# Work of a routed attention's start moved into the two stages before it, and its one-hots spread tile by tile in its loop

## The chip, the cores and the metric

The kernel runs on one core of one Trainium2 chip. The metric is the device time of one execution in microseconds (us). Engines: PE (TensorE), DVE (VectorE), ACT (ScalarE), POOL (GpSimd), each with a queue of its own that is worked in order; SP issues DMAs.

## The reference

The model takes x of 32 x 64 rows of 128 numbers through six residual blocks. The change touches the second and the start of the third:

```python
x = x + xattn(layernorm(x), ctx, ctx)                       # 1 cross attention, 16 heads of 64
x = x + linear_attention_and_mlp(layernorm(x))              # 2
x = x + routed_attention(layernorm(x))                      # 3 four experts, top 2
x = x + masked_cross_attention(ctx, ctx, layernorm(x))      # 4
x = x + relative_attention(layernorm(x))                    # 5
x = causal_attention_and_moe(layernorm(x))                  # 6

# 3: per row, 4 router logits; an expert attends among the rows of a sequence that chose it
logits = x @ router_w + router_b
probs  = softmax(logits);  _, top2 = top_k(probs, 2)
for e in range(4):
    member = (top2 == e).any(-1)
    q, k, v = x @ wq[e] + bq[e], x @ wk[e] + bk[e], x @ wv[e] + bv[e]     # 16 heads of 8
    att = softmax(where(member of the key, q k^T * 0.5, -1e9))
    out += where(member, probs[e], 0) * ((att @ v) @ wo[e] + bo[e])
```

## The kernel before

The 2048 rows are 16 tiles of 128 rows (two sequences each). Each block of the model is a stage, a function that writes a straight program for every engine; a barrier of all engines stands between stages. The order in each queue is the order in which the stage's Python code emits it; nothing is rescheduled. Engines wait for each other on semaphores.

`stage_linear` (L735) works eight groups of two tiles in a software pipeline. In step n DVE does `mask(n-1)`, `xnorm(n+1)`, `stats(n+2)`, `divide(n-1)`, `mid(n-2)`; POOL does `scales(n+2)` and `biases(n)` (L879, two additions of 128x256); PE does the products and transposes. `stage_mlp` (L1016) works the same groups: PE `down(n-1)` (L1153), `up(n)` (L1143), `turn(n+1)` (L1134); ACT the GELU; DVE `xnorm`, `squares`, `result`.

`stage_two_attentions` (L1209) joins blocks 3 and 4. Its start, called the prologue here, is everything up to the first score. DVE copies the identity to bf16 (`identb`, L1929), sums it to `onehot` (L1930), makes the layernorm statistics of all 16 tiles (`norm_stats`, L204 and L208), then the normalised rows (L1936); POOL meanwhile clears `Vbd` (L1353) and makes 1/std per group of four tiles. PE first makes the products of the value bias and `wo` (L1414, L1418), then transposes the rows (`turn_rows`, L1426), makes the router logits (`route`, L1432) and the first queries and keys (L1483, L1491). DVE ranks the logits and writes one-hots `hot` and `out2` (L1949, L1950). PE transposes them (L1441) and `selections` (L1450) spreads them: 48 small products with the constant `place` give, for all 16 tiles, `selT` (which of the four experts' query columns is slot k's) and `neg` (the mask of keys outside). ACT and DVE copy these out of PSUM in six pieces of 128x1024 (`slots`, `outside`: L1759, L1764, L1926). Then the loop runs over n = 0..31, tile t = n // 2, slot k = n % 2: `score(n)` on PE (L1517 adds the mask, L1524 the products) from `Qs` (POOL, L1287) and `RK` (POOL, L1296); `shift(n)` on DVE (L1826 maximum, L1829 subtraction); `exp(n)` on ACT (L1718); `turn(n)` on PE (L1536), `tcopy(n)` on ACT (L1709), `mix(n)` on PE (L1555), `normalise(n)` on DVE (L1913 to L1919). Queries (L1483), keys (L1491) and values (L1501) of tile t+2 and t+1 are made on the way; queries and keys share one PSUM bank, `M`. Output products are `out` (L1568) and `oturn` (L1578).

## Time and profile before

| | us |
|---|---|
| three runs | 1083.43, 1086.52, 1085.63; median 1085.63 |
| the profiled execution | 1082.82, of which the span of its trace is 1081.0 |
| mean granted TensorE clock over the span | 0.948 of full speed |

| stage or stretch | from, to (us of the span) |
|---|---|
| linear attention | 315.5 to 365 |
| MLP | 365 to 393 |
| prologue up to the logits | 394 to 411.5 |
| prologue from the logits to the first score's maximum | 411.5 to 430.54 |
| the loop's first two tiles | 430.54 to 449.2 |
| the loop after that, to the hand-over to block 4 | 449.2 to 600 |

PE is busy in 89% of the span, DVE in 61%, ACT in 48%, POOL in 43%. In the page's 40 slices of 27 us, PE is busy 9 tenths in slices 3 to 10 and 17 onward, but 8, 6, 8, 6, 6 and 6 tenths in slices 11 to 16, which hold the linear stage, the MLP and the prologue. A row of the trace's timeline is a run of like instructions of one engine: its start, the time from its first start to its last end, the instruction, and in brackets the idle time before it and what ended that.

### The profile page before, as it was taken

How to read it: one execution, taken by the hardware profiler on the slowest of the kernel's cores; microseconds unless marked ns; L12 is line 12 of the kernel's file. 1: busy time of each engine (PE TensorE's matmuls, PEld its weight loads, DVE VectorE, ACT ScalarE, POOL GpSimd, SP SyncE). 2: the span in 40 equal slices, each digit the busy share in tenths (PEclk: the TensorE clock that was granted, in tenths of full speed). 3: DMA queues.
4: the chain of work that ended last, by engine and by line, in shares of the span. 5: the costliest groups of instructions: out<-in, count | busy, mean ns of one | idle time of the engine just before them, and what ended most of it. 6: DMA issues, size and time to landing. Idle time of an engine off the chain costs nothing. (4 is left out here: it accounts for less than half of the span.)

```text
span 1081.0 us, 26837 instructions
## 1 busy us (share of the span) xinstructions
PE 960.3 (89%) x10835; PEld 731.7 (68%) x10835; DVE 661.1 (61%) x1314; ACT 515.2 (48%) x1059; POOL 461.4 (43%) x516
## 2 busy tenths in 40 slices
PE   4899999999868666999999999997899788699994
PEld 4788888888556555888888666664355546567773
DVE  3355555555427554688889788884689757622324
ACT  2464555555415323566565556663555438242231
POOL 1123233322225353577677544423144267346243
PEclk9999999999979886899999999998999889699998
DMA  8300033000000010000000000002964010012336
GB/s 274 141 2 1 1 98 101 1 1 1 1 0 1 1 40 1 2 2 2 3 2 3 2 2 2 2 2 97 368 205 113 2 42 4 17 58 62 90 107 180
DMA packets 43369, 55.04 MB, mean 51 GB/s; under 512 B 4368, under 2 KB 34704, under 8 KB 42864
## 3 DMA queue, kind: packets, MB, share of 16 engines
q1 hardware_dynamic: 41264, 49.07, 14.5%
q0 software_dynamic: 1984, 4.26, 1.1%
q8 instruction: 87, 1.43, 0.6%
q14 instruction: 34, 0.28, 0.1%
HBM read 30.13 MB, written 23.19 MB: 49 GB/s over the span
## 5 line engine op out<-in xcount | busy, mean ns | idle before, releaser
L549 POOL TENSOR_TENSOR c_P<-c_P,c_rl 128x1024 f32<-128x1024 f32 x32 | 60.7, 1896 | 127.8 <-DVE c_rl L705 127.8
L1709 ACT COPY e_PT<-probsT 128x512 f32<-128x512 f32 x128 | 69.0, 591 | 96.8 <-PE probsT L1536 96.8
L602 PEld LDWEIGHTS mixed<-c_xs,c_AQ 128*128 128x128 f32 x512 | 66.4, 198 | 35.1 <-issue 33.4
L702 DVE TENSOR_REDUCE c_rl<-c_P 128x8 f32<-128x1024 f32 x32 | 39.0, 1220 | 81.9 <-ACT c_P L364 81.9
L1718 ACT ACTIVATE e_P<-e_P 128x512 f32<-128x512 f32 x128 | 74.6, 640 | 3.4 <-DVE e_P L1829 3.1
L602 PE MATMUL mixed<-c_xs,c_AQ 128*128 128x128 f32 x512 | 71.6, 286 | 2.9 <-ACT c_GT L667 1.6
L626 PE MATMUL mixed<-c_PT,c_cs 128*128 128x512 f32 x128 | 68.6, 618 | 4.5 <-ACT c_RT L676 3.1
L1536 PE MATMUL probsT<-W,e_P 128*128 128x128 f32 x512 | 69.1, 279 | 0.0
L676 ACT COPY c_RT<-mixed 128x512 f32<-128x512 f32 x64 | 37.5, 586 | 62.8 <-PE mixed L626 62.8
L636 PE MATMUL mixed<-c_VO,c_RT 128*128 128x128 f32 x512 | 62.5, 282 | 2.0 <-ACT c_RT L676 2.0
L636 PEld LDWEIGHTS mixed<-c_VO,c_RT 128*128 128x128 f32 x512 | 60.8, 198 | 5.0 <-ACT c_RT L676 5.0
L612 PE MATMUL scores<-ctxT,c_GT 128*128 128x128 f32 x512 | 63.3, 277 | 0.0
L353 DVE TENSOR_REDUCE c_mx<-scores 128x8 f32<-128x1024 f32 x32 | 38.5, 1204 | 39.0 <-PE scores L612 39.0
L612 PEld LDWEIGHTS scores<-ctxT,c_GT 128*128 128x128 f32 x512 | 59.6, 192 | 2.3 <-issue 2.3
L1536 PEld LDWEIGHTS probsT<-W,e_P 128*128 128x128 f32 x512 | 57.1, 142 | 1.5
L386 ACT COPY c_PT<-probsT 128x512 f32<-128x512 f32 x64 | 34.3, 593 | 41.5 <-PE probsT L376 41.5
L667 ACT COPY c_GT<-mixed 128x256 f32<-128x256 f32 x128 | 41.4, 375 | 26.7 <-PE mixed L602 26.7
L1826 DVE TENSOR_REDUCE e_mx<-scores 128x16 f32<-128x1024 f32 x32 | 39.1, 1221 | 21.2 <-PE scores L1524 21.0
L1627 PEld LDWEIGHTS mixed<-x_V,e_PT 128*64 128x64 f32 x1024 | 32.5, 138 | 26.4 <-ACT e_PT L1709 25.6
L1868 DVE TENSOR_REDUCE e_mx<-scores 128x8 f32<-128x1024 f32 x32 | 39.0, 1218 | 15.4 <-PE scores L1607 14.9
L2911 POOL DMA_INDIRECT hbm_results<-e_yo,e_ids x30 | 28.8, 960 | 44.1 <-DVE e_yo L2886 38.6
L2069 POOL TENSOR_TENSOR u_RK<-u_KT,W 128x1024 f32<-128x1024 f32 x16 | 30.4, 1902 | 39.1 <-PE scores L2146 36.3
(391 smaller groups left out, 2374.0 us busy)
## 6 DMA issues: line engine op xcount, KB each, us to landing
hbm_dist<-u_Z SPq DMA_DIRECT2D x16, 768.0 KB, 7.3
u_S<-hbm_dist SPq DMA_DIRECT2D x64, 128.0 KB, 2.8
hbm_results<-c_blank SPq DMA_DIRECT2D x1, 3072.0 KB, 14.2
e_w<-in_w SPq DMA_DIRECT2D x12, 256.0 KB, 2.8
e_dT<-hbm_results SPq DMA_DIRECT2D x12, 256.0 KB, 4.3
W<-in_wpack SPq DMA_DIRECT2D x1, 2489.0 KB, 12.6
hbm_slots<-c_blank SPq DMA_DIRECT2D x6, 350.0 KB, 6.2
e_xin<-hbm_slots SPq DMA_DIRECT2D x6, 350.0 KB, 3.7
```

The costliest lines, as they stand in the source:

```text
L549: pool.tensor_tensor(pr, pr, bc(rl[:, a.up, :].unsqueeze(2), [P, PAIRS, KEYS]), ALU.mult).then_inc(s["scaled"], 1)
L602: last = pe.matmul(bank[:, (h % 4) * P:(h % 4 + 1) * P], AQ[:, h, :], xs[:, a.par, :], start=True, stop=True)
L612: last = pe.matmul(K.psS[a.up][:, c * KEYS:(c + 1) * KEYS], GT[:, a.par, a.u, 2 * c:2 * c + 2, :].rearrange("p h q -> p (h q)"), K.ctxT[:, ...
L626: pe.matmul(K.psO[:, :], cs[:, a.up, :], at.PT[:, a.up, r * 512:(r + 1) * 512], start=True, stop=True).then_inc(s["read"], 1)
L636: last = pe.matmul(K.psO[:, 0:D], RT[:, a.par, h, :], VO[:, h, :], start=(h == 0), stop=(h == HEADS - 1))
L667: last = act.copy(GT[:, a.par, b, 4 * r:4 * r + 4, :], bank[:, :].rearrange("p (h b q) -> p h b q", h=4, b=TB)[:, :, b, :])
L702: dve.tensor_reduce(rl[:, a.up, :], at.P[:, a.up, :].rearrange("p (g k) -> p g k", g=PAIRS), AX.X, ALU.add).then_inc(s["chain"], 1)
L1536: last = pe.transpose(K.psT[:, i * P:(i + 1) * P], Pr[:, n % 2, i * P:(i + 1) * P], K.ident)
L1709: act.copy(PT[:, n % 2, half * 512:(half + 1) * 512], K.psT[:, half * 512:(half + 1) * 512]).then_inc(s["tcopied"], 1)
L1718: act.activation(Pr[:, n % 2, cols], Pr[:, n % 2, cols], ACT.Exp, scale=0.5 if n < TOTAL else CSCALE).then_inc(s["exped"], 1)
L1826: dve.tensor_reduce(top, sc, AX.X, ALU.max).then_inc(s["maxed"], 1)
L1868: dve.tensor_reduce(top, sc, AX.X, ALU.max).then_inc(s["maxed"], 1)
```

## The change

Work is moved from the prologue into the loops of the two stages before, and the spreading of the one-hots from the prologue into the attention's loop.

- In `stage_linear`: DVE makes `onehot` after step 2 and `identb` after step 4. POOL makes `pairmask`, the ones of `V1` and zeros of `hot` after `biases` of step 2, clears `Vbd` after step 3, writes its ones after step 4 and `place` after steps 5 and 6.
- In `stage_mlp`: PE transposes the value bias first and makes the four bias products after step 1; ACT copies in between; DVE finishes the bias rows after step 3. DVE makes the statistics of tiles 0 to 11 after steps 2, 4 and 6 and the normalised rows of tiles 0 to 7 after steps 4 and 6; POOL makes 1/std after steps 3, 5 and 7.
- In the prologue only the statistics of tiles 12 to 15 and the normalised rows of tiles 8 to 15 are left. `keys(0)` goes to another bank and is made before `queries(0)`. `hot` holds the two slots and the mask of each tile beside each other, so that the three one-hots of a tile lie in the same 32 partitions.
- `selections(t)` is now three products and one ACT copy of 128x384 for each tile: tiles 0 and 1 in the prologue, tile t+2 in the loop after `score(2t+1)`, in the bank `M`. `queries(t+2)` comes after that copy and so after `out` and `mix`. On ACT the copy stands after `exp(2t)`, ahead of `values(t)`.

```diff
+                    if a.n == 2:
+                        dve.tensor_reduce(K.onehot[:, :], K.ident.rearrange("p (r i) -> p i r", r=4), AX.X, ALU.add).then_inc(
+                            s["onehot"], 1)
+                    if a.n == 4:
+                        dve.tensor_copy(K.identb[:, :], K.ident)
...
+                def constants(n):
+
+                    if n == 2:
+                        blocks = w("blockmask").rearrange("p (a b) -> p a b", b=2)
+                        pool.tensor_tensor(K.pairmask[:, :], blocks[:, 0, :], blocks[:, 1, :], ALU.add)
+                        pool.memset(K.V1[:, :, :, :, HD:HD + 1], 1.0)
+                        pool.memset(K.hot[:, :, :, :], 0.0)
+                    if n == 3:
+                        pool.memset(K.Vbd[:, :, :, :, :, :], 0.0).then_inc(s["zeroed"], 1)
+                    if n == 4:
+                        for hh in range(2):
+                            pool.wait_ge(s["zeroed"], hh + 1)
+                            pool.memset(K.Vbd[64 * hh:64 * hh + 64, :, :, :, hh, E0 * HD].rearrange("p x b c -> p (x b c)"),
+                                        1.0).then_inc(s["zeroed"], 1)
+                        pool.wait_ge(s["zeroed"], 3)
+                    if n in (5, 6):
+                        pool.wait_ge(s["onehot"], 1)
+                        for j in (2 * (n - 5), 2 * (n - 5) + 1):
+                            pool.tensor_copy(K.place[:, :, j, :, :],
+                                             bc(K.onehot[:, :].rearrange("p (i e) -> p i e", e=E0).unsqueeze(3), [P, 8, E0, HD]))
...
                     biases(a)
+                    constants(a.n)
...
+                def next_stats(g):
+
+                    dve.wait_ge(s["ya"], 2 * (g + 1))
+                    group_stats(dve, v, st6, mv, K.X, g)
+
+                def next_rows(g):
+                    dve.wait_ge(v["rstd"], g + 1)
+                    for t in range(4 * g, 4 * g + 4):
+                        dve.tensor_scalar(K.Xmid[:, t, :], K.X[:, t, :], mv[:, t, 0:1], rstd[:, t:t + 1], ALU.subtract, ALU.mult)
+
+                def bias_rows():
+                    dve.wait_ge(v["bvo"], 1)
+                    dve.tensor_tensor(K.boe[:, :, :], K.psM[:, :].rearrange("p (e d) -> p e d", e=E0),
+                                      row("bo").rearrange("p (e d) -> p e d", e=E0), ALU.add)
...
                     result(a.plus(-1))
+                    if a.n in (2, 4, 6):
+                        next_stats(a.n // 2 - 1)
+                    if a.n == 3:
+                        bias_rows()
+                    if a.n in (4, 6):
+                        next_rows(a.n // 2 - 2)
...
+                def next_scale(g):
+                    tiles = slice(4 * g, 4 * g + 4)
+                    pool.wait_ge(v["var"], g + 1)
+                    pool.tensor_scalar(rstd[:, tiles], mv[:, tiles, 1], LN_EPS, None, ALU.add).then_inc(v["vareps"], 1)
+                    pool.wait_ge(v["vareps"], g + 1)
+                    pool.tensor_tensor(rstd[:, tiles], rstd[:, tiles], K.nhalf[:, tiles], ALU.pow).then_inc(v["rstd"], 1)
...
                     residual(a)
+                    if a.n in (3, 5, 7):
+                        next_scale((a.n - 3) // 2)
...
+                act.wait_ge(v["bvT"], 1)
+                act.copy(bvb[:, :, :], K.psO[:, :].rearrange("p (e d) -> p e d", e=E0)).then_inc(v["bvb"], 1)
...
+                def bias_products():
+                    pe.wait_ge(v["bvb"], 1)
+                    for e in range(E0):
+                        last = pe.matmul(K.psM[:, e * P:(e + 1) * P], bvb[:, e, :], w("wo", e * D, D), start=True, stop=True)
+                    last.then_inc(v["bvo"], 1)
...
+                    if a.n == 1:
+                        bias_products()
+
+                for e in range(E0):
+                    last = pe.transpose(K.psO[:, e * P:(e + 1) * P], row("bv", e * D, D), K.ident)
+                last.then_inc(v["bvT"], 1)
...
+            selected = lambda t: (M if t else K.psT)[:, 0:(TOPK + 1) * P]
+            keyed = lambda t: M if t else K.psO
...
-                        if t == 0:
-                            pool.wait_ge(q["selout"], 1)
+                        pool.wait_ge(q["selout"], t + 1)
...
-                    blocks = w("blockmask").rearrange("p (a b) -> p a b", b=2)
-                    pool.tensor_tensor(pairmask[:, :], blocks[:, 0, :], blocks[:, 1, :], ALU.add).then_inc(q["pair"], 1)
-                    pool.memset(Vbd[:, :, :, :, :, :], 0.0).then_inc(q["zeroed"], 1)
-                    pool.wait_ge(q["zeroed"], 1)
-                    for hh in range(2):
-                        pool.memset(Vbd[64 * hh:64 * hh + 64, :, :, :, hh, E0 * HD].rearrange("p x b c -> p (x b c)"), 1.0).then_inc(
-                            q["zeroed"], 1)
-                        pool.wait_ge(q["zeroed"], hh + 2)
-                    for g in range(groups):
-                        tiles = slice(g * G, (g + 1) * G)
-                        pool.wait_ge(q["var"], g + 1)
-                        pool.tensor_scalar(rstd[:, tiles], mv[:, tiles, 1], LN_EPS, None, ALU.add).then_inc(q["vareps"], 1)
-                        pool.wait_ge(q["vareps"], g + 1)
-                        pool.tensor_tensor(rstd[:, tiles], rstd[:, tiles], K.nhalf[:, tiles], ALU.pow).then_inc(q["rstd"], 1)
-
-                    pool.memset(V1[:, :, :, :, HD:HD + 1], 1.0).then_inc(c["ones"], 1)
-                    pool.wait_ge(q["onehot"], 1)
-                    for j in range(4):
-                        pool.tensor_copy(place[:, :, j, :, :], bc(onehot[:, :].rearrange("p (i e) -> p i e", e=E0).unsqueeze(3),
-                                                                  [P, 8, E0, HD])).then_inc(q["place"], 1)
-                    pool.wait_ge(q["pair"], 1)
...
+                    def selections(t):
+
+                        if t >= TILES:
+                            return
+                        if t == 0:
+                            pe.wait_ge(q["hotTout"], 1)
+                        else:
+                            pe.wait_ge(s["qout"], t)
+                            pe.wait_ge(s["kout"], t)
+                        rows = slice(32 * (t % 8 // 2), 32 * (t % 8 // 2) + 32)
+                        for kind in range(TOPK + 1):
+                            last = pe.matmul(selected(t)[:, kind * P:(kind + 1) * P],
+                                             place[rows, 4 * (t % 2) + kind, :, :, :].rearrange("p j e d -> p (j e d)"),
+                                             hotT[rows, t // 8, :], start=True, stop=True)
+                        last.then_inc(q["sel"], 1)
 
                     def queries(t):
                         if t >= TILES:
                             return
-                        wait(pe, s["kout"], t)
+                        if t:
+                            pe.wait_ge(q["selout"], t + 1)
...
+                        if t == 0:
+                            pe.wait_ge(s["kout"], 1)
...
-                    biases()
                     turn_rows(0)
                     turn_rows(1)
                     route(0)
+                    keys(0)
                     queries(0)
-                    turn_rows(2)
                     route(1)
-                    turn_rows(3)
-                    route(2)
-                    route(3)
-                    keys(0)
+                    for g in range(2, groups):
+                        turn_rows(g)
+                    for g in range(2, groups):
+                        route(g)
+                    turn_hot()
+                    selections(0)
+                    values(0)
+                    selections(1)
                     queries(1)
-                    selections()
+                    score(0)
                     keys(1)
-                    values(0)
-                    pe.wait_ge(q["selout"], 2)
-                    score(0)
                     for n in range(TOTAL):
                         t, u = divmod(n, U)
-                        if n == 0:
-                            pe.wait_ge(q["selout"], 4)
-                            pe.wait_ge(q["selout2"], 2)
                         score(n + 1) if n + 1 < TOTAL else wide_score(0)
                         if u == 0:
-                            queries(t + 2)
+                            selections(t + 2)
                             out(t - 2)
                             mix(n - 1)
+                            queries(t + 2)
                             turn(n)
...
+                    def selections(t):
+                        if t >= TILES:
+                            return
+                        act.wait_ge(q["sel"], t + 1)
+                        act.copy(sel[:, t, :, :], selected(t).rearrange("p (k q) -> p k q", k=TOPK + 1)).then_inc(q["selout"], 1)
...
+                        if g == 1:
+                            keys(0)
...
                     act.activation(ex[:, :, :], ex[:, :, :], ACT.Exp).then_inc(q["exped"], 1)
-                    keys(0)
                     act.wait_ge(q["hotT"], 1)
-                    act.copy(hotT[:, :, :], K.psO[:, 0:2 * P].rearrange("p (i q) -> p i q", i=2)).then_inc(q["hotTout"], 1)
-                    slots(0, K.psT[:, :], 1)
-                    outside(0, K.psS[0][:, :], 2)
-                    slots(2, K.psT[:, :], 4)
-                    outside(2, K.psT[:, :], 6)
+                    act.copy(hotT[:, :, :], K.psT[:, 512:512 + 2 * P].rearrange("p (i q) -> p i q", i=2)).then_inc(q["hotTout"], 1)
+                    selections(0)
+                    values(0)
+                    selections(1)
                     keys(1)
...
                         exp(n)
-                        if u == 0 and t >= 1:
-                            values(t)
+                        if u == 0:
+                            selections(t + 2)
+                            if t >= 1:
+                                values(t)
...
+                    for t in range(TILES - G, TILES):
+                        last = dve.bn_stats(st6[:, t, :], K.X[:, t, :])
+                    last.then_inc(q["stats"], 1)
+                    dve.wait_ge(q["stats"], 1)
+                    for t in range(TILES - G, TILES):
+                        last = dve.bn_aggr(mv[:, t, :], st6[:, t, :])
+                    last.then_inc(q["var"], 1)
+                    for g in range(DONE, groups):
+                        rows_ready(g)
...```

PE's queue at the start of the joined attentions, up to the first scores (`W` and `R` are the packed weights and rows; `mixed`, `scores`, `probsT` are PSUM). Before:

```order
L1414 MATMUL probsT<-W,R 128x128 x4
L1418 MATMUL probsT<-W,e_wb 128x128 x4
L1426 MATMUL scores<-W,Xmid 128x128 x8
L1432 MATMUL mixed<-W,XnT 128x4 x4
L1483 MATMUL mixed<-XnT,W 128x128 x4
L1426 MATMUL scores<-W,Xmid 128x128 x4
L1432 MATMUL mixed<-W,XnT 128x4 x4
L1426 MATMUL scores<-W,Xmid 128x128 x4
L1432 MATMUL mixed<-W,XnT 128x4 x8
L1491 MATMUL mixed<-XnT,W 128x128 x4
L1483 MATMUL mixed<-XnT,W 128x128 x4
L1441 MATMUL mixed<-x_identb,e_hot 128x128
```

PE's queue at the same place after the change:

```order
L1471 MATMUL scores<-W,Xmid 128x128 x8
L1477 MATMUL probsT<-W,XnT 128x4 x4
L1521 MATMUL mixed<-XnT,W 128x128 x4
L1512 MATMUL mixed<-XnT,W 128x128 x4
L1477 MATMUL probsT<-W,XnT 128x4 x4
L1471 MATMUL scores<-W,Xmid 128x128 x8
L1477 MATMUL probsT<-W,XnT 128x4 x8
L1485 MATMUL probsT<-e_identb,e_hot 128x128 x2
L1501 MATMUL probsT<-e_hotT,e_place 128x128 x3
L1533 MATMUL mixed<-W,XnT 64x4x8x8 x4
L1501 MATMUL mixed<-e_hotT,e_place 128x128 x3
L1512 MATMUL mixed<-XnT,W 128x128 x4
```

The bias products are gone from the head, both sets of transposes stand closer together, and six spreading products stand where 48 followed.

PE's queue in one even step of the loop (n = 2t), from its score to its transposes. Before:

```order
L1517 MATMUL scores<-e_neg,e_selT 64x512 x4
L1524 MATMUL scores<-e_RK,e_Qs 64x128 x16
L1483 MATMUL mixed<-XnT,W 128x128 x4
L1568 MATMUL scores<-W,e_oT 128x8x16 x4
L1555 MATMUL scores<-e_Vbd,e_PT 64x2x33 x16
L1536 MATMUL probsT<-W,e_P 128x128 x8
```

PE's queue in the same step after the change:

```order
L1549 MATMUL scores<-e_sel 64x512 x4
L1556 MATMUL scores<-e_RK,e_Qs 64x128 x16
L1501 MATMUL mixed<-e_hotT,e_place 128x128 x3
L1602 MATMUL scores<-W,e_oT 128x8x16 x4
L1589 MATMUL scores<-e_Vbd,e_PT 64x2x33 x16
L1512 MATMUL mixed<-XnT,W 128x128 x4
L1570 MATMUL probsT<-W,e_P 128x128 x8
```

Three products are new, and the queries moved behind `out` and `mix`.

POOL's queue in steps 3 and 4 of the linear stage after the change (before, L879 was followed by the next L866, with nothing between):

```order
L890 TENSOR_TENSOR Xmid<-Xmid,l_projB 128x256
L890 TENSOR_TENSOR X<-X,l_downB 128x256
L900 MEMSET e_Vbd 128x2112
L877 TENSOR_SCALAR l_rs<-l_mv 128x2
L879 TENSOR_SCALAR l_rs<-l_mv 128x2
```

The clearing of `Vbd`, which stood at the head of the prologue, now follows the two additions of step 3.

## Rows read from the trace of the kernel before

**Rows 1.** Engines' busy time by stretch: start:end, length, busy of PE, PEld, DVE, ACT, POOL, PEclk, DMA.
```profile
315.50:365.00 49.50, 35.92 (x208) 25.98 (x208) 34.11 (x140) 22.97 (x64) 23.04 (x40) 0.93 0.00 1
365.00:393.00 28.00, 21.26 (x112) 16.88 (x112) 11.46 (x57) 10.52 (x25) 13.18 (x24) 0.88 0.00 1
394.00:411.50 17.50, 12.67 (x69) 11.77 (x70) 10.82 (x52) 4.06 (x6) 8.80 (x17) 0.61 0.22 61
411.50:430.54 19.04, 11.81 (x118) 8.59 (x117) 9.08 (x25) 8.09 (x17) 6.19 (x5) 0.55 0.00 0
449.20:600.00 150.80, 149.35 (x2527) 125.64 (x2527) 130.48 (x177) 93.41 (x202) 112.14 (x112) 1.00 0.01 3
```
**Rows 2.** Timeline of the prologue: start, us, engine, line, instruction, idle before.
```profile
394.04 2.05 DVE L1929 CAST x_identb<-W 128x128 bf16<-128x128 f32 x1 [1.24 <-PEq L143]
394.16 1.86 POOL L1353 MEMSET e_Vbd<- 128x2112 f32 x1
394.51 3.65 DVE L204 BATCH_NORM_STATS2 e_st<-X 128x6 f32<-128x128 f32 x16
...
401.30 1.12 PE L1426 MATMUL scores<-W,Xmid 128*128 128x128 f32 x4 [3.88 <-DVE Xmid L1936]
...
403.34 1.83 PEld L1432 LDWEIGHTS mixed<-W,XnT 128*128 128x128 f32 x8
405.12 2.05 PE L1483 MATMUL mixed<-XnT,W 128*128 128x128 f32 x8
...
411.50 0.23 DVE L1942 TENSOR_TENSOR e_logits<-mixed,R 128x64 f32<-128x64 f32 x1 [3.60 <-PE mixed L1432]
...
414.00 1.92 DVE L1950 TENSOR_SCALAR e_out<-e_rank 128x128 bf16<-128x128 f32 x1
416.41 0.37 ACT L1775 CAST e_hotT<-mixed 128x256 bf16<-128x256 f32 x1 [2.66 <-PE mixed L1441]
417.16 0.92 PEld L1450 LDWEIGHTS scores<-e_hotT,e_place 32*128 32x128 bf16 x16
421.05 0.69 DVE L1815 TENSOR_TENSOR e_QT<-mixed,biasE 128x512 f32<-128x512 f32 x1 [4.53 <-POOL e_Qs L1287]
424.25 0.61 PE L1450 MATMUL scores<-e_hotT,e_place 32*128 32x128 bf16 x8 [5.06 <-DVE e_selT L1926]
427.22 1.98 PE L1501 MATMUL mixed<-W,XnT 128*64 128x256 f32 x8
429.30 1.19 ACT L1745 COPY e_Vbd<-mixed 64x512 f32<-64x512 f32 x2 [0.83 <-PE mixed L1501]
430.54 1.23 DVE L1826 TENSOR_REDUCE e_mx<-scores 128x16 f32<-128x1024 f32 x1 [4.41 <-PE scores L1524]
```
**Rows 3.** Timeline of the linear stage, DVE and POOL.
```profile
340.86 0.73 POOL L879 TENSOR_TENSOR X<-X,l_downB 128x256 f32<-128x256 f32 x1
341.62 0.34 DVE L801 TENSOR_SCALAR l_xn<-X,l_mv,l_rs 128x128 f32<-128x128 f32 x1
343.66 0.19 DVE L825 TENSOR_SCALAR l_den<-probsT 128x32 f32<-128x32 f32 x1 [0.51 <-PE probsT L987]
350.95 0.75 DVE L801 TENSOR_SCALAR l_xn<-X,l_mv,l_rs 128x128 f32<-128x128 f32 x1
```
**Rows 4.** Timeline of the MLP stage, PE and DVE.
```profile
377.19 0.47 DVE L1053 TENSOR_SCALAR m_xn<-Xmid,m_rs 128x128 f32<-128x128 f32 x2
380.10 0.38 PE L1134 MATMUL scores<-W,m_xn 128*128 128x128 f32 x2
380.82 1.16 PE L1153 MATMUL probsT<-downG,m_hT 128*128 128x128 f32 x8 [0.34 <-ACT m_hT L1117]
```
**Rows 5.** Timeline of one tile of the attention's loop.
```profile
456.35 0.97 PEld L1483 LDWEIGHTS mixed<-XnT,W 128*128 128x128 f32 x8 [0.17 <-issue]
458.33 1.15 PE L1555 MATMUL scores<-e_Vbd,e_PT 128*64 128x66 f32 x32
460.11 1.07 ACT L1709 COPY e_PT<-probsT 128x512 f32<-128x512 f32 x2 [3.08 <-PE probsT L1536]
```

150 lines of the change are left out of this document (49 added, 101 removed).

## The prediction

> **What bounds the kernel now.** I read the slices first: PE is busy 9 tenths or more in most of them, and dips in slices 11 to 16. The table of busy times by stretch says what lies there. In the loop of the joined attentions PE is busy 149.35 of 150.80 us at full clock, and no other engine more than 130.48: whatever is added to PE's queue there is paid in full. In the prologue PE is busy 12.67 of 17.50 and 11.81 of 19.04 us, at a granted clock of 0.61 and 0.55 [rows 1]: a chain of waits at mostly half speed (1.2 GHz). In the linear stage neither PE (35.92 of 49.50) nor DVE (34.11) is full.
>
> The timeline of the prologue shows the chain [rows 2]. DVE's first instruction, a cast that needs a fraction of a microsecond, takes 2.05 because POOL clears `Vbd` for 1.86 beside it; then come 16 statistics (3.65), aggregates, POOL's 1/std and the rows. PE gets its first transposes at 401.30, waits for ACT's copy, and works through logits products (1.83 for a group), queries (2.05) and the rest at half clock; DVE has the logits at 411.50. The mask one-hots are issued at 414.00 and take 1.92, the transposed one-hots are cast at 416.41 and spread from there, and PE then sits 5.06 until 424.25 on a DVE copy, because DVE itself waited 4.53 at 421.05 (its queries of tile 1 need `QT` free, which POOL reads). The first score's maximum starts at 430.54, which is 36.5 us after the stage's first instruction at 394.04. The timeline of the linear stage shows a cycle of DVE and PE: DVE is idle only 0.51 in a unit, before the division [rows 3]. The loop of the MLP is PE's, with 0.34 of idle in a unit, waiting for ACT [rows 4].
>
> **The prologue: -12.2 us.** Statistics of 12 tiles, rows of 8, bias products, `Vbd`, `identb`, `onehot` and 42 of 48 spreading products leave it. PE starts with transposes at once. Its queue to the logits is, at half clock: 16 transposes in four groups of about 0.9 (four take 1.12 with the last one's latency), four groups of logits products at 1.83, keys and queries at 2.05 each, and 0.6 of waiting for a copy (two take 1.07 on ACT [rows 5]): 3.6 + 7.3 + 4.1 + 0.6 = 15.6 [rows 2]. At full clock (keys or queries 0.97 [rows 5], two transposes 0.38 [rows 4]) it is half of 15.0 and about 1.0 of waits, 8.5. DVE's own part is hidden under PE: the way from the first statistic to 401.30 took 6.8 us with 16 statistics (3.65) and POOL's clearing; with 4 of them it ends before 399, and PE wants these rows after 400. PE is now nearly unbroken, and in 394 to 411.5 it had 0.61, so I take 11.4, logits at 405.4.
>
> From there: 2.5 of DVE's ranking (411.50 to 414.00), 0.2 for the mask (its 1.92 had POOL's `RK` beside it; with `keys(0)` early that is over by 403), 0.95 for transposing and casting `hot` (415.92 to 416.78, and 0.1 to PE): tile 0's selections are issued at 409.1. Behind them PE does `values(0)` (1.98, to 411.4), ACT its two copies (1.19, to 412.7) and the cast for tile 1 (0.5, between 0.37 for 256 columns and 0.59 for 512), 413.3; then `queries(1)` 2.05 to 415.5, and the score 1.5 (1.34 from the end of L1501 to 430.54, and a gap): maximum at 417.0 [rows 2]. Gain 430.54 - 417.0 = 13.5. The ends: everything at full clock gives 412.8 (17.7), everything at half clock 420.6 (10). POOL's `Qs` of tile 0 starts at 410.2 and is hidden under `values` and `queries`. Of it 1.3 is given back in the first step: `queries(2)` (2.05) now stands between the cast behind `exp(0)` and `turn(0)`, and only part of it is covered by `exp(0)`. Ends 0.5 and 2.
>
> **The linear stage: +3.1 us.** What is put at the end of DVE's step is in the cycle: `onehot` 0.25 (128 numbers in, and the 128x64 addition of rows 2 takes 0.23), `identb` 0.2. POOL has room, but what it does beside DVE is not free: at 350.95 `xnorm` takes 0.75 instead of 0.34 while POOL starts one of its 0.73 additions [rows 3], and the cast of rows 2 took the whole clearing. The clearing comes after `biases(3)`, whose addition runs 340.86 to 341.59; DVE's `xnorm(5)` has its second instruction at 341.62 [rows 3], so it waits out the 1.86: +1.7. The small ones (`hot`, ones, `place`, `identb` against an addition) are seven chances of 0.1 to 0.4; I take 0.95 in all. Sum 0.45 + 1.7 + 0.95 = 3.1; ends 1.0 (clearing slips between DVE's instructions) and 5.0 (all collide). The Trainium skill (GPSIMD Engine Reference, Specifications) says that POOL shares its SBUF interfaces with DVE and contends with instructions in a two-port mode or with two SBUF inputs. By that the casts and `xnorm` are exposed and the reduction is not, so `onehot` would cost 0.25 wherever POOL is; by the cast's row, were it to hold for reductions too, up to 1.9.
>
> **The MLP: +0.7 us.** The four transposes and ACT's copy lie in the wait for the first rows. The bias products cost 0.97, less the idle 0.34 they stand in: 0.6. DVE gets some 7 us in all (12 statistics and aggregates 4, rows 2.2, the bias rows 0.7), and is busy 11.46 of 28.00 [rows 1]; after steps 4 and 6 it gets 2.5 at once, a backlog of 1.2, but `xnorm(4)` is made at 377.19 for a transpose at 380.10, 2.4 us of slack [rows 4]. So nothing, or 0.1. Ends 0.3 and 2.5 (the backlog comes out, or the products fall in half clock).
>
> **The loop: +4.6 us.** 14 tiles get three products of 128 columns in bf16. 16 such took 0.92 at half clock, 0.058 each, but in two groups of partitions in turn [rows 2]; now all three of a tile are in the same 32, so I take twice that at half and 0.055 at full clock, 0.16 a tile. Before L1483, where the products' tile size changes from 64*64 to 128*128, PE's loads stand 0.17 for no one [rows 5]; the new products have a third size, and so one such gap more: 0.33 a tile, 4.6. Ends: 0.16 (2.2) and 0.50 (7.0). The Trainium skill (TensorEngine Tiling (Array Packing), Key Properties) says that changing the tiling mode drains TensorE while tiles of one mode run in parallel. The trace agrees with 0.17 at the change; by the rule the 4.6 stands, and were it not for the drain 2.2 would.
> The order is otherwise harmless: `mix` starts at 458.33; without the queries ahead of it (0.9) and with the selections (0.33) it starts at 457.8, and PE reaches `queries(t+2)` at 458.9. The cast they wait for starts when the products are done, about 456.8, and ends at 457.3, since ACT, idle for 3.08 before 460.11, did `values(t)` (1.19) from 455.8 and `exp(2t)` before that [rows 2, 5]. `values(t)` on ACT slips by 1.3 into the same idle time.
>
> **Sum.** -12.2 + 3.1 + 0.7 + 4.6 = -3.8. The profiled execution took 1082.82 (span 1081.0 and 1.8 around it), so it would be 1079.0; it lies 2.8 below the median of the three, and I forecast against the median: 1085.6 - 3.8 = **1081.8**.
>
> **Rivals.**
> 1. *PE keeps the full clock in the prologue.* It is fed without a break from 394, and in rows 1 the low mean goes with long waits. Against: `route` products have 4 columns, and DVE's ranking still stops PE for 3 us. Then 17.7 - 0.5 - 8.4 = 8.8: 1076.8. 0.20.
> 2. *Slower: the queries wait for ACT.* On ACT the cast stands behind `exp(2t)`. If in the new rhythm `exp(2t)` ends later than 458.3 (458.9 less the cast and 0.1), PE stands in front of `queries(t+2)` with `turn` behind it. Now it ends at 455.8, so it decides from 2.5 us later on; each 0.1 beyond costs 1.4 over 14 tiles, the gain is gone at 0.27 a tile (3.8), and 0.6 a tile costs 8.4: 1090.2. For it: `M` is now shared by three, and DVE, whose `shift` sets exp, is busy 130 of 151. Against: those 2.5 us. 0.12.
> 3. *Stalled DVE starves PE and the clock falls.* In the linear stage 0.93 means some 7 us at half clock. One more such stretch in the MLP, PE's own, costs 3.4: 1085.2, no change. 0.18.
>
> **How the numbers follow.** The forecast has 0.50, its own range 1078.5 to 1084.5. What a measurement can tell from no change is 0.3%, 3.3 us; -3.8 lies just beyond, so 0.30 of the 0.50 is faster and 0.20 the same. Rival 1 is all faster. Rival 3 gives 0.15 same and 0.03 slower, rival 2 0.01 and 0.11. Faster 0.50, same 0.36, slower 0.14. The bounds of all terms at once are -13.9 and +6.4; eight in ten: 1075.5 to 1088.
>
> **What would show it.** From the stage's first instruction to the first score's maximum: 23 us (36.5 before); 19 if rival 1 holds. An `xnorm` instruction of about 2 us beside the clearing. In the loop a PE period of 11.5 for a tile instead of 11.2 (150.8 us for 13.5 tiles) with no wait of the queries on ACT; a wait there is rival 2. The forecast is wrong if the linear stage loses over 5, or the loop's period grows by more than 0.5.

## The result, and the profile after

| | before | after |
|---|---|---|
| median of six runs, us | 1085.98 (1083.43 to 1088.65) | **1073.43** (1071.02 to 1077.80) |
| the profiled execution | 1082.82, span 1081.0 | 1074.42, span 1072.3 |
| mean granted clock of that execution | 0.948 | 0.950 |

The ratio, here and below that of the mean times, is 0.9888, 95% interval 0.9865 to 0.9910: 12 us faster. Forecast were 1081.8 and a range from 1075.5 to 1088.0, so the time lies below the range. The direction was right; the gain is three times the forecast one. One execution of the many reported here, of the kernel with its bias products back in the prologue, took 1161.53 us at a mean granted clock of 0.817 and is left out of that kernel's numbers; all others ran at 0.935 or more.

The two profiled executions lie only 8.7 us of span apart. Before's took 3.2 us less than the median of its six runs, after's 1.0 more than that of its own. I come back to this, since it is part of the answer.

These are the busy times of after by stretch, with the columns and the stages of [rows 1]: linear stage, MLP, prologue to the logits, logits to first maximum, loop.

```profile
315.80:369.70 53.90, 39.51 (x208) 28.77 (x208) 35.10 (x139) 23.05 (x64) 26.92 (x50) 0.84 0.00 1
369.70:398.00 28.30, 21.97 (x124) 17.10 (x124) 19.13 (x91) 11.28 (x26) 17.13 (x30) 0.87 0.01 1
398.00:409.70 11.70, 11.37 (x64) 10.85 (x64) 4.07 (x17) 4.67 (x9) 3.16 (x3) 0.65 0.34 91
409.70:421.90 12.20, 7.60 (x61) 5.08 (x62) 4.41 (x22) 2.76 (x6) 2.26 (x2) 0.51 0.00 0
449.00:600.00 151.00, 150.34 (x2513) 125.21 (x2511) 125.12 (x174) 96.96 (x207) 109.00 (x110) 1.00 0.01 3
```

Against [rows 1] the linear stage is longer and has a clock of 0.84 in place of 0.93. The MLP took 7.67 us more of VectorE at nearly the same length. The prologue to the logits has PE busy 11.37 of 11.70 us (12.67 of 17.50 before), and the stretch behind it is 12.2 us in place of 19.04. The timeline of after's prologue, against [rows 2] (start, length, engine, line, instruction, idle before):

```profile
398.08 0.87 DVE L1960 BATCH_NORM_STATS2 n_st<-X 128x6 f32<-128x128 f32 x4 [1.29 <-PEq L143]
398.08 1.94 PE L1471 MATMUL scores<-W,Xmid 128*128 128x128 f32 x8 [1.75 <-PEq L143]
...
401.58 2.05 PE L1521 MATMUL mixed<-XnT,W 128*128 128x128 f32 x8
...
409.73 0.23 DVE L1971 TENSOR_TENSOR e_logits<-probsT,R 128x64 f32<-128x64 f32 x1 [3.99 <-PE probsT L1477]
...
412.91 0.37 ACT L1803 CAST e_hotT<-probsT 128x256 bf16<-128x256 f32 x1 [2.15 <-PE probsT L1485]
...
413.76 1.98 PE L1533 MATMUL mixed<-W,XnT 128*64 128x256 f32 x8
...
417.00 0.48 ACT L1793 CAST e_sel<-mixed 128x384 bf16<-128x384 f32 x1
...
417.53 2.08 PE L1512 MATMUL mixed<-XnT,W 128*128 128x128 f32 x8 [1.36 <-ACT e_sel L1793]
...
421.88 1.23 DVE L1853 TENSOR_REDUCE e_mx<-scores 128x16 f32<-128x1024 f32 x1 [1.55 <-PE scores L1556]
```

PE starts on transposes with the stage, as forecast. From the stage's first instruction (398.05) to the logits it is 11.7 us (forecast 11.4, before 17.5), and to the first maximum 23.8 (forecast 23, before 36.5). The queries of tile 1 wait 1.36 us for ACT's cast. In the linear stage, against [rows 3], the clearing does what was forecast:

```profile
343.17 2.09 DVE L805 TENSOR_SCALAR Xmid<-X,l_mv,l_rs 128x128 f32<-128x128 f32 x1
343.33 1.86 POOL L900 MEMSET e_Vbd<- 128x2112 f32 x1
343.42 1.90 DVE L807 TENSOR_SCALAR l_xn<-X,l_mv,l_rs 128x128 f32<-128x128 f32 x1
...
345.89 0.44 PE L977 MATMUL scores<-W,l_xn 128*128 128x128 f32 x2 [2.11 <-DVE l_xn L807]
346.26 1.03 PE L1020 MATMUL probsT<-l_KV,l_phq 128*64 128x144 f32 x8
347.22 1.22 PE L1031 MATMUL mixed<-l_projG,l_oT 128*128 128x128 f32 x4
```

Two row instructions stand until POOL is done, PE idles 2.11 us, and then PE's products take 1.03 and 1.22 us where the unit before has 0.71 for each line. The trace's record of the clock has 0.5 from 346.5 to 349.9: a consequence that my 1.7 us did not contain. In the MLP, against [rows 4], the bias products stand with their 1.06 us, but the stage is not longer:

```profile
378.85 1.06 PE L1228 MATMUL mixed<-W,m_bvb 128*128 128x128 f32 x8
```

In the loop, against [rows 5]:

```profile
456.03 1.04 PE L1556 MATMUL scores<-e_RK,e_Qs 64*64 64x128 f32 x32
...
457.00 0.17 PEld L1501 LDWEIGHTS mixed<-e_hotT,e_place 32*128 32x128 bf16 x3 [0.17 <-issue]
457.00 0.34 PE L1501 MATMUL mixed<-e_hotT,e_place 32*128 32x128 bf16 x3
...
457.38 0.48 ACT L1793 CAST e_sel<-mixed 128x384 bf16<-128x384 f32 x1 [0.76 <-PE mixed L1501]
...
459.44 1.16 PE L1512 MATMUL mixed<-XnT,W 128*128 128x128 f32 x8
...
468.47 0.17 PEld L1501 LDWEIGHTS mixed<-e_hotT,e_place 32*128 32x128 bf16 x3 [0.17 <-issue]
```

The products of a tile and the gap of 0.17 us ahead of them are there; from 457.00 to 468.47 is one tile, 11.47 us (11.16 before). The cast ends at 457.86, the queries start at 459.44 without a wait: rival 2 did not come.

### The ledger

I cut the profiled execution of each kernel into the same six pieces, at five points of the timeline. A is the last addition of the cross-attention to `X`; B the last sum into `Xmid`; C the first instruction of the attention stage; D the third of the loop's maxima; E the last of its 32. "Half" is the time in that piece at a granted clock of 0.5.

| profile | A | A-B linear (half) | B-C MLP (half) | C-D prologue, first tile (half) | D-E loop | E-end | span |
|---|---|---|---|---|---|---|---|
| before | 313.1 | 51.4 (6.8) | 29.5 (6.8) | 46.7 (37.5) | 160.9 | 479.4 | 1081.0 |
| before, second profile | 313.2 | 51.4 (6.8) | 29.8 (10.2) | 48.8 (41.0) | 160.9 | 480.8 | 1085.0 |
| after | 312.7 | 56.7 (17.1) | 28.7 (7.2) | 31.8 (20.1) | 164.0 | 478.5 | 1072.3 |
| after, second profile | 309.7 | 56.0 (17.1) | 30.1 (10.2) | 28.5 (13.7) | 164.0 | 479.9 | 1068.3 |

First pair: -0.5 + 5.3 - 0.7 - 14.9 + 3.0 - 0.9 = -8.7 us. The loop is the same to 0.1 us in both profiles of a kernel; what is left moves with the half clock, also where no instruction was changed: ahead of A after's two profiles have 6.8 us of it and none (312.7 and 309.7), behind E 56.8 and 60.3 us (478.5 and 479.9).

### The profile page after: what moved, and what is told of

Its sections match the earlier page's. It is cut to its first block and busy times, and to the rows that moved or that the text cites. A ratio compares the mean times of both kernels' runs of the same rounds, so it can differ in the third digit from the quotient of the medians.

```text
span 1072.3 us, 26858 instructions
## 1 busy us (share of the span) xinstructions
PE 960.8 (90%) x10835; PEld 730.2 (68%) x10835; DVE 658.4 (61%) x1312; ACT 519.3 (48%) x1071; POOL 462.0 (43%) x517
## 5 line engine op out<-in xcount | busy, mean ns | idle before, releaser
L676 ACT COPY c_RT<-mixed 128x512 f32<-128x512 f32 x64 | 37.5, 586 | 63.1 <-PE mixed L626 63.1
L1570 PE MATMUL probsT<-W,e_P 128*128 128x128 f32 x512 | 67.5, 275 | 0.0
L1570 PEld LDWEIGHTS probsT<-W,e_P 128*128 128x128 f32 x512 | 57.0, 141 | 0.6
L1853 DVE TENSOR_REDUCE e_mx<-scores 128x16 f32<-128x1024 f32 x32 | 39.2, 1224 | 25.4 <-PE scores L1556 25.4
L1661 PEld LDWEIGHTS mixed<-e_V,e_PT 128*64 128x64 f32 x1024 | 32.5, 138 | 26.4 <-ACT e_PT L1741 25.6
```

The costliest lines, as they stand in the source:

```text
L1570: last = pe.transpose(K.psT[:, i * P:(i + 1) * P], Pr[:, n % 2, i * P:(i + 1) * P], K.ident)
L1853: dve.tensor_reduce(top, sc, AX.X, ALU.max).then_inc(s["maxed"], 1)
```

## The experiments

Theory: the mechanisms of the prediction are all there, and what was mis-sized is the clock. TensorE's idle time in before's prologue costs more than itself, since the products behind it then run at half clock. Rival 1: all of it is scatter. Rival 2: single parts (statistics, loop, clearing) have other prices than I gave them. Every ratio is to the kernel before in runs on the same chip; after's own were 0.9888 and, in a second set, 0.9899, in the mean 0.9894, which I take as the reference. C-D and the other letters are those of the ledger.

### Both kernels again

> The changed kernel again, unchanged. Its first profile ended 8.4 us before the profile of the kernel before (1074.42 against 1082.82), the medians 12.5 us apart. Theory A (the difference is scatter of the granted clock from run to run: the profile of before fell on a good run, that of after on a middling one): the new median lies within 1071 to 1077, the loop's period stays 11.48 us per tile to within 0.02, and the stretches at half clock in the linear stage (13.7 us at its start in after's first profile, 6.8 in before's) differ between this profile and the first one of the same kernel. Theory B (the long stretch at half clock in the linear stage is caused by the change): it is there again, 13 to 14 us long, and mask to mask the second unit again takes 5.7 us against 4.4.

Measured: 1071.68 us (1068.30 to 1076.00), ratio 0.9899 (0.9876 to 0.9922). The loop's period is 11.47 again. The 13.7 us at half clock at the start of the linear stage came again too, as theory B had it; the kernels below settle it. Two with after's linear stage (doubled products, spreads ahead) had 6.8 there, and the filled kernel before, whose code is before's up to the attentions, had 13.7. So that stretch is no doing of the change, and theory A holds: C-D had 13.7 us at half clock in place of 20.1 and was 3.3 us shorter.

> The kernel before again, for a second profile of it. Its first one took 1082.82 us, under all six timed runs then (1083.43 to 1088.65). Theory A (scatter of the granted clock from run to run): period of the loop 11.16 us per tile again and the logits again 17 to 18 us after the attention stage's first instruction, while the stretches at half clock in the linear stage, the MLP and the prologue of the attentions lie or last differently, and the stage lengths differ by the same amounts. Theory B: all stages as in the first profile to 0.3 us.

Measured: one execution, 1087.09 us, theory A. The loop and the linear stage are the same to 0.1 us, but the logits come 19.7 us after the start, not 17 to 18, and C-D is 2.1 us longer. PE's timeline shows the place, in before's first profile

```profile
409.56 1.89 PE L1432 MATMUL mixed<-W,XnT 128*128 128x4 f32 x16
411.32 1.25 PE L1491 MATMUL mixed<-XnT,W 128*128 128x128 f32 x8
```

and in its second:

```profile
410.67 3.41 PE L1432 MATMUL mixed<-W,XnT 128*128 128x4 f32 x16
413.94 2.06 PE L1491 MATMUL mixed<-XnT,W 128*128 128x128 f32 x8
```

The same 16 logits products and the keys take 3.0 us or 5.3 us. The execution from which I predicted had a stretch at full clock there (408.8 to 412.2 us); the other had none from 395.9 to 433.5.

### The kernel before, with TensorE's idle time filled

```diff
                     biases()
+                    for i in range(4):
+                        pe.matmul(K.psS[0][:, 0:512], K.ident, w("wq"), start=True, stop=True)
                     turn_rows(0)
...
                         slots(2, K.psT)
+                        for i in range(5):
+                            pe.matmul(K.psO[:, 0:512], K.ident, w("wq"), start=True, stop=True)
                         pe.wait_ge(q["selout2"], 1)
```

> The kernel BEFORE with TensorE given products without use in two places of the prologue where its queue stands idle: four of 128x512 behind the bias products (idle 397.4 to 401.3 in its first profile), five of 128x512 behind the selections' third group (idle 419.2 to 424.25). Nothing else is changed. In before's two profiles the granted clock was 0.5 over most of the prologue, and where one had a stretch at 1.0 (408.8 to 412.2) its logits came 17.5 us after the stage's first instruction against 19.7 in the other. Theory A (the half clock comes of TensorE's own idle time at the stage's start, and costs the prologue of before some 3 to 6 us over what its instructions take at full clock): the stretches at 0.5 get shorter by 7 us or more between the stage's start and the third maximum, the third maximum comes 43 us or less after the start (46.7 and 48.8 in the profiles of before), total 2 to 6 us less than before, 1079 to 1083. Theory B (the clock does not follow this, or only much later): half clock as before, the products fill idle time only, total within 1.5 us of before's, or up to 3 us more if they run longer than the gaps.

Measured: 1078.30 us against 1085.70, ratio 0.9936 (0.9913 to 0.9959). Nine products whose results nobody reads make the kernel before 7 us faster. C-D of before's first profile, by engine:

```profile
394.00:440.70 46.70, 31.91 (x275) 26.72 (x276) 25.39 (x80) 15.21 (x28) 18.81 (x25) 0.60 0.08 23
```

and of the filled kernel:

```profile
392.00:433.10 41.10, 34.91 (x293) 25.61 (x294) 23.61 (x81) 14.95 (x28) 17.96 (x24) 0.79 0.10 27
```

PE's timeline of the filled kernel:

```profile
395.24 4.36 PE L1649 MATMUL scores<-W 128*128 128x512 f32 x8
399.43 0.60 PE L1426 MATMUL scores<-W,Xmid 128*128 128x128 f32 x4
...
401.98 1.14 PE L1485 MATMUL mixed<-XnT,W 128*128 128x128 f32 x8
```

The stretch is 5.6 us shorter although the products without use fill 10.4 us of it; PE's own products take about 24.5 us of its busy time in place of 31.9; the clock's mean rises from 0.60 to 0.79; four transposes take 0.60 in place of 1.12 and the queries 1.14 in place of 2.05 [rows 2]. Half clock falls from 37.5 and 41.0 us to 17.1. Theory A, and more than its 2 to 6 us. So TensorE's idle time makes before's prologue slow beyond its own length. It is not what brings the clock down: in the first profile of before the clock is 0.5 from 395.1 and from 412.2 us, ahead of both filled waits (397.4 and 419.2). It falls in the filled kernel too, at 393.3 and 407.0, but there it is back after 3.4 and 10.2 us, and in before after 13.7 and 17.1. What the waits do is keep it down. The two fills were not tried one by one, so how much each brings is not shown. After, with its shorter waits, has 20.1 and 13.7 us at half clock.

### Statistics back in the prologue

All of `next_stats`, `next_scale` and `next_rows` leave the MLP, and the prologue makes 16 tiles' statistics and rows as before (`DONE = 0`).

> The changed kernel with statistics, powers and rows of all four groups back in the prologue of the attentions; bias products, constants and the per-tile spreading stay as in after. It prices the statistics alone. Theory A (the prologue's first part is VectorE's chain: statistics of 16 tiles, power, rows): logits 3.5 to 5 us later than the 11.5 us after the stage's first instruction in after, MLP stage 0 to 0.7 us shorter, total +3.5 to +5, near 1076.5. Theory B (the router's wait is set by TensorE at half clock, which runs behind VectorE anyway): logits later by less than 2 us, total within 2 us of after's 1072.5.

Measured: 1082.34 us, ratio 0.9974 (0.9952 to 0.9996): +8.7 us on after, twice theory A. The MLP is no shorter without them: 30.2 us with 10.2 at half clock, as after's second profile (30.1). The statistics are free there. The timeline of this kernel's prologue:

```profile
396.10 3.19 DVE L204 BATCH_NORM_STATS2 n_st<-X 128x6 f32<-128x128 f32 x16 [1.29 <-PEq L143]
...
402.36 1.12 PE L1466 MATMUL scores<-W,Xmid 128*128 128x128 f32 x4 [8.01 <-DVE Xmid L1949]
...
416.68 0.23 DVE L1959 TENSOR_TENSOR e_logits<-probsT,R 128x64 f32<-128x64 f32 x1 [6.02 <-PE probsT L1472]
```

PE stands 8 us, the clock is then 0.5 for 30.7 us without a break, and the logits are at 20.6 us after the start (8.3 and 11.7 in after). I had counted VectorE's chain alone, at 3.5 to 5 us. That was short by itself, since PE's first transposes come 6.3 us after the stage's first instruction and in after at once; the 10.6 to 17.0 us more at half clock come on top. How the 8.7 us divide between the two is not shown.

### Bias products back in the prologue

The transposes of `bv`, ACT's copy, the four products (into `M`) and VectorE's sum stand ahead of `turn_rows(0)` again.

> The changed kernel with the bias products (four transposes, a copy on ACT, four products of 128x128 and VectorE's sum) back at the start of the attentions' prologue, all else as in after. It prices this part alone. In before these stood on TensorE beside VectorE's statistics of 16 tiles (TensorE idle 3.9 us behind them). Theory A (with the statistics gone TensorE is no longer waiting there, so the products are exposed): about 3.4 us at the prologue's start (0.63 + 0.67 + 2.07 at half clock, as in before's trace), the first maximum at 27 us after the stage's start in place of 23.8, MLP stage unchanged to 0.3 us; total +3 to +4.5, near 1076. Theory B (the router's chain on VectorE and ACT sets the first score, and TensorE has slack in front): within 1 us of after's 1072.5.

Measured: 1077.60 us, ratio 0.9929 (0.9894 to 0.9964), +3.9 us; first maximum 27.5 us after the start. Theory A. In before they cost nothing, since PE waited for the statistics anyway:

```profile
399.83 2.07 PE L1664 MATMUL mixed<-W,e_wb 128*128 128x128 f32 x8 [0.67 <-ACT e_wb L1784]
401.69 1.92 PE L1451 MATMUL scores<-W,Xmid 128*128 128x128 f32 x8
```

Here the transposes of rows that have been ready for long stand behind them.

### All selections ahead of the first score

```diff
+                    for t in range(1, TILES):
+                        selections(t)
-                    selections(1)
                     queries(1)
                     score(0)
...
                         if u == 0:
-                            selections(t + 2)
                             out(t - 2)
```

> The changed kernel with all 16 tiles' selections spread ahead of the first score, as the kernel before had them (there in six groups shared by ACT and VectorE, here tile by tile with ACT's casts alone, alternately in the halves of probsT); the rest as in after. It splits the change: what spreading in the loop brings and costs. Theory A (the loop's spreading costs 0.3 us per tile, and the spreads ahead cost the prologue their casts, 15 x about 0.6 us less what lies beside the second queries and POOL's products): the period falls from 11.47 to 11.16, 4.4 us over 14 tiles, the first maximum comes 7 to 9 us later, total +3 to +5, near 1076. Theory B (the loop's longer period has another cause, as the queries moved behind the mix): the period stays above 11.3 and the total rises by 7 us or more, to 1079 and above.

Measured: 1076.12 us, ratio 0.9928 (0.9905 to 0.9951), +3.7 us. Period 11.21 (theory A: 11.16), first maximum 6.8 us later than in after's first profile, D-E 161.0 us. Spreading in the loop costs 3.0 us there and saves 6.6 (C-D 38.5 against 31.8, with 27.0 against 20.1 us at half clock). Theory A. The 0.05 us per tile that stay may be the queries' place behind the mix.

### The loop's products doubled

```diff
-                        for kind in range(TOPK + 1):
+                        for kind in (0, 1, 2, 0, 1, 2) if t > 1 else (0, 1, 2):
```

> In the loop, the three spreading products of tiles 2 to 15 are issued twice, back to back into the same place (14 x 3 products more). It prices the loop's term, which the prediction put together of 0.16 us for three products and 0.17 us for a gap where TensorE goes over to 32 rows of weights. Theory A (gap per group): the period per tile rises from 11.48 by 0.16, 14 tiles 2.2 us in all, 1075.7. Theory B (the whole 0.3 is paid per product, as latency or weight loads): 0.3 per tile, 4.3 us in all, 1077.7. Theory C (what the loop pays is the cast of the selections on ACT and the wait of the queries for it): no change, 1073.4, or a wait of more than 0.1 us before the queries in each tile.

Measured: 1076.16 us, ratio 0.9931 (0.9905 to 0.9956); period 11.64, D-E 166.0 against 164.0 us. The timeline:

```profile
466.62 0.33 PEld L1501 LDWEIGHTS mixed<-e_hotT,e_place 32*128 32x128 bf16 x6 [0.17 <-issue]
466.62 0.50 PE L1501 MATMUL mixed<-e_hotT,e_place 32*128 32x128 bf16 x6
```

Three products more cost 0.17 us and no second gap: theory A. The split of the loop's term, 0.16 and 0.17 of 0.31 to 0.32 us measured, was right. The ratio says +4.1 us for the kernel, near theory B's 4.3, and the loop explains only 2.0 of it. In the profile the rest lies behind E, where nothing was changed: 480.9 us with 64.7 at half clock, against 478.5 and 479.9 in after. So theory A rests on the loop's period, not on the total.

### The clearing out of the linear stage

```diff
-                    if n == 3:
-                        pool.memset(K.Vbd[:, :, :, :, :, :], 0.0).then_inc(s["zeroed"], 1)
...
                     pool.tensor_tensor(rstd[:, last], rstd[:, last], K.nhalf[:, last], ALU.pow).then_inc(q["rstd"], 1)
+                    pool.memset(Vbd[:, :, :, :, :, :], 0.0).then_inc(q["zeroed"], 1)
```

(with its two fills of ones, and ACT's first `values` waiting for them).

> The clearing of Vbd (1.86 us on POOL) and its ones (2 x 0.36/2) leave the linear stage and stand on POOL in the prologue of the joined attentions, behind the last group's power, where POOL idles 400.8 to 404.9 in the trace of after. Theory A (in the linear stage the clearing holds up two VectorE row instructions, 2.09 and 1.90 us in place of 0.34, TensorE idles 2.11 us and the clock then falls once): the linear stage is 1.6 us shorter by the hold alone, up to 3.0 if the fall of the clock at 346.5 goes with it; in the prologue the clearing falls beside the row instructions of the last group (1.11 us for four), which end about 1.9 us later, at 403.8, still ahead of TensorE's turn at 405.6: nothing lost. Total -1.6 to -3.0 us, near 1071. Theory B (the hold was covered, or the prologue gives it back): within 0.5 us of after; then the first scores' maximum lies later than 23.8 us after the stage's first instruction by what the linear stage won.

Measured: 1070.14 us (1068.90 to 1070.69), ratio 0.9873 (0.9857 to 0.9889), -2.2 us on after. A-B is 52.1 us against 56.0 and 56.7, with no half clock behind unit 3. Of the kernels with the clearing left in, those whose clock did not fall behind it (doubled products, spreads ahead) have 53.4 with the same start as this one: the hold alone is 1.3 us. The rest goes with half clock, at the stage's start and behind the hold. In the prologue the clearing holds the last four rows, for which PE has no use yet:

```profile
395.55 1.86 POOL L1422 MEMSET e_Vbd<- 128x2112 f32 x1
395.63 2.43 DVE L1955 TENSOR_SCALAR Xmid<-X,n_mv,n_rstd 128x128 f32<-128x128 f32 x4 [0.47 <-POOL n_rstd L1421]
...
400.63 1.07 PE L1469 MATMUL scores<-W,Xmid 128*128 128x128 f32 x8
```

They end at 398.1, and their transposes start at 400.6. Theory A.

### The prologue in another order

```diff
-            selected = lambda t: (M if t else K.psT)[:, 0:(TOPK + 1) * P]
+            selected = lambda t: K.psT[:, 512 * t:512 * t + (TOPK + 1) * P] if t < 2 else M[:, 0:(TOPK + 1) * P]
...
+                    values(0)
                     turn_hot()
                     selections(0)
-                    values(0)
                     selections(1)
                     queries(1)
```

> Prologue only: the first tile's values stand ahead of the turn of the one-hots, where TensorE idles 409.7 to 412.5 in after's trace, and the second tile's selections get a half of probsT of their own, so that the second queries no longer wait for their cast (0.7 to 1.4 us). Theory A (after the router's chain TensorE's own queue sets the first score: values 1.98, wait 1.36, queries 2.08): the first score starts at about 416.8 in place of 419.5, the first maximum 21 us after the stage's first instruction in place of 23.8, total -2.7 us, near 1070.7. Theory B (the loop's start is set by POOL's products and the exponentials, or the fuller TensorE in front of them changes when the clock rises): the first maximum comes earlier, but the third one, 31.8 us after the stage's start in after, by less than 1 us, and the total stays within 1 us of after's.

Measured: 1070.75 us (1066.45 to 1075.15), ratio 0.9884 (0.9858 to 0.9910): by the ratio -1 us, within the scatter, so the total does not bear out theory A's -2.7. Its profile has A, A-B, B-C, the logits (8.3 us after the start) and the loop as after's second profile has them, so that C-D can be compared: 25.1 us against 28.5. In the profile it is theory A, 3.4 us in place of 2.7:

```profile
403.95 1.98 PE L1533 MATMUL mixed<-W,XnT 128*64 128x256 f32 x8
...
407.66 0.82 PE L1501 MATMUL probsT<-e_hotT,e_place 32*128 32x128 bf16 x6 [0.47 <-ACT e_hotT L1804]
...
408.41 2.08 PE L1512 MATMUL mixed<-XnT,W 128*128 128x128 f32 x8
...
410.41 0.64 PE L1549 MATMUL scores<-e_sel 64*64 64x512 bf16 x4
```

The values lie in the wait for the one-hots, the queries start without their 1.36 us of waiting.

### Both edits: a version faster than both kernels

> Both edits tried singly before: the clearing of Vbd in the attentions' prologue on POOL, and the first tile's values ahead of the one-hots' turn with the second tile's selections in probsT. In the single runs' profiles the first shortened the linear stage by 2.9 us (41.65 to 38.73 from the first masked KV to the last sum), the second brought the first maximum 3.6 us earlier (416.44 to 412.84). Theory A (independent): linear stage 38.7, first maximum 16 us... that is 12.4 us ahead of that of the kernel before plus 3, at about 412.8; median 1067 to 1069. Theory B (now ACT's copy of the first values waits for POOL's clearing and holds up the cast of the one-hots, which is behind it): the clearing ends at about 403 on after's clock against a copy at 411.8, so this should not be seen; if it is, ACT's copy waits for POOL and the first maximum comes more than 1 us later than in the second edit alone, 1070 or more.

Measured: 1064.17 us (1062.41 to 1072.14), ratio 0.9838 (0.9799 to 0.9877); first maximum at 410.4 in a profile whose stage starts at 391.4, C-D 27.1 us. That is under theory A's 1067 to 1069. And once more:

> The kernel with both edits (clearing on POOL in the attentions' prologue, the first values ahead of the one-hots' turn) once more, as the reference of the next run on the same chip and for the size of its gain: its first median was 1064.17 against 1085.23 of before (0.9838). Theory A (the gain is of the kernel, not of the runs it happened to get): 1063 to 1067 again. Theory B (scatter): 1068 or more.

Measured: 1067.28 us (1065.16 to 1071.01) against 1085.72, ratio 0.9839 (0.9808 to 0.9870), just over theory A's 1067 in time and the same in ratio. 6 us faster than after. The two alone brought 2.2 and 1.0 by the ratios (2.2 and 3.4 with the second by its profile); the interval of this ratio is 3 to 4 us wide to each side, so that the two together bring more than their sum is not shown.

### The same cure in the linear stage

To the version with both edits, at the start of the linear stage:

```diff
+                for i in range(5):
+                    pe.matmul(K.psM[:, :], K.ident, w("wq"), start=True, stop=True)
                 turn(At(0, 0, 1))
```

> The same kernel, with five products without use (128x512, about 1.1 us each at full clock by the eight records in 4.36 us of the four in the filled kernel before) on TensorE at the very start of the linear stage, where it waits 6.5 us for VectorE's first rows (309.2 to 315.7) and its clock is then 0.5 from 312.0 to 325.7. Theory A (as in the attentions' prologue: idle TensorE is what costs the clock): most of the 13.7 us at half clock go, the first masked KV comes 1.5 to 3 us earlier after the first row statistics, total -1.5 to -3 us against the kernel without them. Theory B (the linear stage's first units are set by VectorE, POOL and ACT, or the clock falls all the same): no change within 1 us, or the products, still running when the first rows come, cost up to 1 us.

Measured: 1068.13 us (1064.45 to 1072.02), ratio 0.9842 (0.9809 to 0.9874): no gain, which is theory B for the total. The stage itself behaves as theory A has it. A-B in the kernel without the products, and then with them:

```profile
311.20:363.40 52.20, 36.30 (x208) 26.27 (x208) 36.05 (x146) 22.98 (x64) 24.95 (x47) 0.93 0.00 1
```

```profile
312.90:363.20 50.30, 38.72 (x218) 26.73 (x218) 36.09 (x148) 22.98 (x64) 24.95 (x47) 1.00 0.00 1
```

Full clock throughout and 1.9 us less. But its MLP took 30.3 us against 29.4, its prologue had 20.5 us at half clock against 17.1, and C-D was 30.1 against 28.2. Whether the first causes the second, or the two profiles only differ as before's two do, stays open: one profile each doesn't tell.

## Why the prediction was wrong in size

The mechanisms of the four terms are in the traces, and the direction was right. The step that failed is the size of the prologue's term, -12.2 us, which measured -16.8: the waits that leave it were priced as idle time, at the clock of one mild execution, and not by the half clock that they prolong. The loop's and the MLP's costs were put too high as well, by 1.6 and 1.2 us.

**The prologue, -12.2: too small.** In the first pair of profiles the parts up to the first maximum were right: logits 11.7 after the start (11.4 forecast), first maximum 23.8 (23), so 12.7 gained to there of the 13.5. The logits' bound for full clock, 8.5, came in after's second profile, with 8.3 at a clock of 1.0. What failed stands behind the first maximum: "1.3 is given back in the first step". On balance 2.2 more were gained up to the third maximum, because before's scores, queries and transposes of that stretch ran at half clock for 6.8 of 10.2 us and after's at full clock (1.0 from 421.6 on). PE did wait 0.57 us for the cast there, so the new order has a price that the clock hides. C-D is -14.9 in the first pair. And the execution that I predicted from was a mild one. Over the profiles with the same prologue, C-D is 47.8 us in the mean of two (before) and 31.0 in the mean of four (after twice, clearing moved, products doubled): **-16.8**. Of these, 15.2 are gained up to the first maximum (38.2 against 22.9 us after the start), and 1.6 behind it, where 1.3 were to be given back. Rival 1 (PE keeps the full clock, 19 us to the first maximum) had 0.20, and I argued against it with the waits that remain. The second profile of after, with 20.6 us, lies between it and the forecast, but it did not come as it stands: 13.7 to 20.5 us of those four stretches are at half clock.

**The clock as a cost of waiting.** In [rows 1] I read 0.61 and 0.55 as a state of the stretch and priced what was removed by its instructions. The filled kernel shows that PE's 3.88 and 5.06 us of waiting [rows 2] prolong it, and that this is worth 7 us of before's time. How much of the change's own 12 us comes that way and how much from fewer instructions was not separated.

**The linear stage, +3.1: +5.3 in the first pair, +2.0 where the clock stayed up.** The `xnorm` instruction of 2 us is there (2.09), the cost of the hold 1.3 us (1.7 forecast). The small ones are mostly free: `onehot` took 0.37 us at 337.21 beside one of POOL's additions, near the 0.25 forecast and far from the 1.9 of the other bound, `identb` 0.22 (0.50 in after's second profile). By the rule that I took from the Trainium skill (GPSIMD Engine Reference, Specifications) the row instructions are exposed to POOL and the reduction is not, and these rows agree, as far as they go. No run has the reduction alone beside the clearing. In before it stood beside it, behind the cast, with 1.88 us:

```profile
394.22 1.88 DVE L1930 TENSOR_REDUCE e_onehot<-W 128x32 f32<-128x128 f32 x1
```

Cast, reduction and the six statistics issued behind them all end within 0.01 us of each other, at 396.1, so that only the first need have been held and the others stood behind it. The same goes for the two long row instructions of after, which end 0.06 us apart.

Not in the sum was that the 2.11 us in which PE waits bring a stretch at half clock: rival 3, at a place where I had priced the wait alone. With like starts (A at 309.6 and 309.7) the stage takes 56.0 us with the hold and the fall and 53.4 without the clearing (both edits, first profile), 2.6 us. In part the +5.3 is no cost of the change at all: the longer stretch at half clock at the stage's start comes in before's code as well. The filled kernel has it, with A at 309.5 and A-B 52.8 us; against it after's 56.0 is +3.2, close to the 3.1.

**The MLP, +0.7: nothing.** B-C lies between 28.7 and 30.1 us in after and at 29.5 and 29.8 in before, and it is not shorter with the statistics taken out.

**The loop, +4.6: +3.0.** The price per tile was right (11.47 to 11.48 against 11.16, forecast 11.5 against 11.2), and so were its two parts. The multiplication by 14 was not. Between the third and the last maximum lie 13 of the periods, and not each pays: by the distances of the maxima the first two grow by 0.12 and 0.22, one of before's, with 11.70 us, shrinks to 11.48, and the last two, 22.20 us together, grow by 0.09 in all. The step that spreads the third tile's one-hots lies ahead of D. The Trainium skill (TensorEngine Tiling (Array Packing), Key Properties) has the drain at a change of mode; the doubled products, which cost 0.17 a tile and no second gap, bear out that there is one gap for a group.

**The sum against the median.** Over before's two profiles and the four that have after's pieces (for A-B, B-C and both ends: after twice, doubled products, spreads ahead), the means give -16.8 in the prologue, +3.5 in the linear stage, -0.5 in the MLP, +3.0 in the loop, and -1.0 before A and -0.7 behind E, where no instruction was changed: -12.5. The medians say -12.5 and -11.8. Of the 8.7 us between this and the forecast -3.8, the prologue has 4.6, the loop 1.6, the MLP 1.2 and the untouched stretches 1.7, which is luck and was not forecast; the linear stage takes back 0.4. I made the sum from one execution and set it under the median; where executions differ by what the clock does, the gain has to be estimated for the typical one. That before's profiled one was 2.8 us under the median was in view. The bounds of all terms at once also add up to -13.7 and +6.5, not -13.9 and +6.4.

**The rivals.** The queries wait for ACT's cast twice, 1.36 us in the prologue and 0.57 in the loop's first step, and never after. So rival 2's wait exists where the loop begins and has no weight. "No change", with 0.36, did not come.
